# TensorE projects before it forms the output product in the attention steps, and GpSimd splits the weights

## The reference

```python
q = (x @ wq).reshape(B, T, H, Dh)
c_kv = x @ w_down
kv_up = (c_kv @ w_up).reshape(B, T, H, 2 * Dh)
k, v = (kv_up[..., :Dh], kv_up[..., Dh:])
q = _apply_rope(q, 0)
k = _apply_rope(k, 0)
scores = jnp.einsum('bqhd,bkhd->bhqk', q, k) * scale
scores = jnp.where(causal[None, None, :, :], scores, -jnp.inf)
attn = jax.nn.softmax(scores, axis=-1)
out = jnp.einsum('bhqk,bkhd->bqhd', attn, v).reshape(B, T, H * Dh)
return out @ wo
```

## Time and profile before

| | us |
|---|---|
| median of 3 runs (1430.68 to 1434.95) | 1431.06 |
| the profiled execution | 1435.23 |
| its span | 1433.2 |
| TensorE busy in the span | 1360.4 (95%) |
| VectorE busy | 1006.6 (70%) |
| ScalarE busy | 606.8 (42%) |
| GpSimd busy | 564.9 (39%) |

### The profile page before, as it was taken

How to read it: one execution, slowest core, us unless ns; L and a number is a source line. 1 busy time by engine, 2 the same in 40 slices (tenths; PEclk the granted TensorE clock), 3 DMA queues, 4 the chain that set the end, 5 groups by cost and what they waited for, 6 DMA issues and landing times.

```text
span 1433.2 us, 24788 instructions
## 1 busy us (share of the span) xinstructions
PE 1360.4 (95%) x8292; PEld 1114.6 (78%) x8292; DVE 1006.6 (70%) x2533; ACT 606.8 (42%) x1490; POOL 564.9 (39%) x488
## 2 busy tenths in 40 slices
PE   8998999999999999889999999999999999997995
PEld 7777787888888878668877788788788888874664
DVE  5797989898989898865564567566557657886225
ACT  4554555555555555533333343343334333351232
POOL 3775555555555555200124123513513522304122
PEclk9999999999999999999999999999999999988998
DMA  6000000000000200120000010110020001677994
GB/s 187 1 12 1 12 0 11 0 11 0 11 0 11 65 0 1 20 68 1 0 2 0 31 51 9 36 54 9 16 73 7 8 16 41 169 261 242 288 267 133
DMA packets 67952, 76.16 MB, mean 53 GB/s; under 512 B 14189, under 2 KB 55173, under 8 KB 67877
## 3 DMA queue, kind: packets, MB, share of 16 engines
q1 hardware_dynamic: 56533, 58.36, 14.1%
q10 hardware_dynamic: 8560, 12.36, 2.9%
q0 software_dynamic: 2784, 4.46, 1.5%
HBM read 66.22 MB, written 8.95 MB: 52 GB/s over the span
## 4 chain that ended last, share of the span: by engine, by line
PE 39%; DVE 8%; POOL 3%; ACT 3%; issue 2%; DMA 1%; POOLq 0%; ACTq 0%; DVEq 0%
PE ps L1848 28%; PE ps L2215 2%; PE ps L2364 2%; PE ps L2442 1%; PE ps L2205 1%; PE ps L2128 1%; PE ps L2129 1%; PE ps L2133 1%; POOL wq L626 1%; POOL wo L626 1%; DVE hidT L1440 1%; POOL wo L621 0%; POOL wq L621 0%; POOL qk L694 0%; PE ps L2424 0%
## 5 line engine op out<-in xcount | busy, mean ns | idle before, releaser
L863 ACT ACTIVATE probs<-ps,nm 128x128 f32<-128x128 f32 (+3 forms) x256 | 135.3, 529 | 209.2 <-DVE nm L1269 209.2
L694 POOL TENSOR_TENSOR qk<-q,ksb 128x512 f32<-128x512 f32 x64 | 83.5, 1304 | 283.1 <-ACT q L977 210.9
L1994 PE MATMUL ps<-kT,qT 128*128 128x128 f32 (+3 forms) x512 | 160.5, 436 | 8.7 <-ACT probs L863 4.6
L1201 DVE TENSOR_TENSOR prod<-ps,rope_sb 128x1024 f32<-128x1024 f32 x128 | 155.2, 1215 | 7.5 <-PE ps L1848 7.5
L556 POOL TENSOR_TENSOR qT<-prod 64x512 f32<-64x512 f32 x64 | 81.9, 1280 | 144.4 <-DVE prod L1201 134.0
L1178 DVE TENSOR_TENSOR pT_low<-ps,pT 128x384 fp32r<-128x384 f32 (+2 forms) x256 | 104.6, 450 | 44.4 <-ACT pT L783 44.4
L1269 DVE CUSTOM_DVE_ANT_0 ps<-ps,causal 128x128 f32<-128x128 f32 (+3 forms) x256 | 122.5, 499 | 7.6 <-PE ps L1994 7.5
L556 POOL TENSOR_TENSOR kT<-prod 64x512 f32<-64x512 f32 x64 | 81.9, 1279 | 90.7 <-DVE prod L1201 79.4
L1333 DVE SCALAR_TENSOR_TENSOR acc<-ps,rinv,acc 128x256 f32<-128x256 f32 x256 | 105.9, 473 | 1.8 <-issue 1.4
L783 ACT ACTIVATE pT<-ps 128x384 fp32r<-128x384 f32 (+2 forms) x256 | 85.1, 415 | 51.8 <-PE ps L2031 51.4
L1848 PEld LDWEIGHTS ps<-kvo,qn 128*128 128x128 f32 x768 | 100.2, 191 | 8.3 <-DVE qn L1178 3.6
(11 more groups left out here) (298 smaller groups left out, 3066.0 us busy)
## 6 DMA issues: line engine op xcount, KB each, us to landing
eg<-in_L_ffn_w_gate_dram SPq DMA_DIRECT2D x16, 704.0 KB
eg<-in_L_ffn_w_up_dram SPq DMA_DIRECT2D x16, 704.0 KB
ed<-in_L_ffn_w_down_dram ACTq DMA_DIRECT2D x10, 640.0 KB
ksb<-ks_dram SPq DMA_DIRECT2D x16, 256.0 KB, 3.3
ed<-in_L_ffn_w_down_dram SPq DMA_DIRECT2D x6, 640.0 KB
rows_dram<-rows ACTq DMA_DIRECT2D x4, 640.0 KB, 8.1
acc<-in_L_attn_x_dram SPq DMA_DIRECT2D x4, 512.0 KB
wq_in<-in_L_attn_wq_dram SPq DMA_DIRECT2D x8, 256.0 KB, 2.9
```

The lines of the kernel that those rows point to most:

```text
L694: nc.gpsimd.tensor_tensor(qk[:], q3[:], ksb[b % 2][:], ALU.mult).then_inc(qk_ready, 1)
L863: nc.scalar.activation(probs[hh][:, off:off + (i + 1) * P], ps[:, BS + i % 2, 0:(i + 1) * P], ACT.Exp, bias=nm[:, hh, i:i + 1], scale=-1.0 ...
L1201: nc.vector.tensor_tensor(prod[parity][w][:], ps[:, BA:BA + 2, :], rope[:, w:w + 1, :].broadcast_to([P, 2, T]), ALU.mult).then_inc(product ...
L1994: pe.matmul(ps[:, bank, 0:(i + 1) * P], qT[:, hh, b, i * P:(i + 1) * P], kT[:, hh, b, 0:(i + 1) * P], start=True, stop=True).then_inc(scor ...
```

## The change

There are three parts. In the attention's steps, `project` moves in front of `project_out`. Work of splitting moves from ScalarE and VectorE to GpSimd: the rests of wq and wk in every pair but the last, and both halves of all FFN weights, which GpSimd does when its last rotation is done, with root(1) in their midst. The factor SCALE moves from wq to the maxima's pass, the wait for all of U_low in front of the loop becomes one for each pair, the statistics of the first sequence move from n = 2 and 3 to n = 4 and 5, and around the FFN some transposes and copies change places.

```diff
-        w0_pieces = [([h[:, k, w, :] for h in gu], gu_in[:, k, w, :]) for k in range(KD) for w in range(2)]
-        w0_pieces.insert(2, ([h[:] for h in la], la_in[:]))
+        w0_pieces = [([h[:, k, w, :] for h in gu], gu_in[:, k, w, :]) for w in (1, 0) for k in range(KD)]
+        w0_pieces.insert(1, ([h[:] for h in la], la_in[:]))
         w0_pieces.append(([h[:] for h in lb], lb_in[:]))
...
+            def weights_rest(o, whole, hi, turned, ready, count, signal):
+                pool.wait_ge(roped, 4 * turned)
+                pool.wait_ge(ready, count)
+                nc.gpsimd.tensor_tensor(o, whole, hi.bitcast(F32), ALU.subtract).then_inc(signal, 1)
+                pool.wait_ge(signal, count)
...
             def pair(g, first, last):
                 for n in range(STEPS - LOOK if last else STEPS):
                     b = (n + LOOK) // 2 % BATCH
-                    if last and n == 2:
-                        pool.wait_ge(roped, 4 * (g * STEPS + LOOK + n))
-                        root(1)
-                        pool.wait_ge(rstd_ready, 1)
+                    if n == 3 and not last:
+                        weights_rest(wq[1][:], wq_in[:], wq[0][:], g * STEPS + LOOK + n, wq_hi, g + 2, wq_lo)
+                    if n == 4 and not last:
+                        weights_rest(wk[1][:], wk_in[:], wk[0][:], g * STEPS + LOOK + n, wk_hi, g + 2, wk_lo)
...
             pool.wait_ge(roped, 4 * PROJECTIONS)
+            pool.wait_ge(gu_loaded, 32)
+            for m, (halves, whole) in enumerate(w0_pieces):
+                if m == 1:
+                    pool.wait_ge(la_loaded, 8 * 16)
+                if m == 3:
+                    root(1)
+                    pool.wait_ge(rstd_ready, 1)
+                if m == 5:
+                    pool.wait_ge(lb_loaded, 64)
+                one = ones[0:whole.shape[0], :]
+                if len(whole.shape) == 3:
+                    one = one.rearrange("p (a n) -> p a n", a=1)
+                nc.gpsimd.tensor_tensor(halves[0], whole, one.broadcast_to(list(whole.shape)), ALU.mult).then_inc(w0_hi, 1)
+                pool.wait_ge(w0_hi, w0_first + m + 1)
+                nc.gpsimd.tensor_tensor(halves[1], whole, halves[0].bitcast(F32), ALU.subtract).then_inc(w0_lo, 1)
+            pool.wait_ge(w0_lo, w0_first + 6)
             root(2)
             root(3)
...
-                nc.scalar.activation(wq[0][:], wq_in[:], ACT.Copy, scale=SCALE).then_inc(wq_hi, 1)
+                copy(wq[0][:], wq_in[:]).then_inc(wq_hi, 1)
...
                 act.wait_ge(ha_turned, b + 1)
                 copy(haT[:], ps[0:NL, 6, :]).then_inc(haT_ready, 1)
+                if not last:
+                    xa_halves(b + 1)
...
-                nc.vector.tensor_tensor_reduce(out=row, in0=row, in1=causal[:, T - (i + 1) * P:T], scale=-1.0, scalar=-MASKED,
+                nc.vector.tensor_tensor_reduce(out=row, in0=row, in1=causal[:, T - (i + 1) * P:T], scale=-SCALE, scalar=-MASKED,
...
-                if n == 3 and not last:
-                    split_wq(g + 1)
-                if n == 4 and not last:
-                    split_wk(g + 1)
                 if last:
-                    if n == 2:
+                    if n == 4:
...
                         dve.wait_ge(acc_added, 4 * s)
                         statistics(tiles(0), None)
-                    if n == 3:
+                    if n == 5:
                         dve.wait_ge(rstd_ready, 1)
...
-                    if n in w0_lo_at:
-                        for m in w0_lo_at[n]:
-                            halves, whole = w0_pieces[m]
-                            dve.wait_ge(w0_hi, w0_first + m + 1)
-                            rest(halves[1], whole, halves[0]).then_inc(w0_lo, 1)
...
+            dve.wait_ge(w0_lo, w0_first + 6)
             route0(0)
             take_weights()
             o_rest(STEPS * PAIRS - 1)
+            xa_rests(0)
             add(STEPS * PAIRS - 1, STEPS - 1)
-            xa_rests(0)
...
                 scores(2)
                 scores(3)
-                if first and n == 1:
-                    pe.wait_ge(ulo_ready, ulo_first + 1)
+                if n + LOOK < STEPS or not last_pair:
+                    project((n + LOOK) % 2, (n + LOOK) // 2 % BATCH, s + LOOK, g if n + LOOK < STEPS else g + 1)
+                if n == 1:
+                    pe.wait_ge(ulo_ready, ulo_first + g + 1)
                 if not (first and n == 0):
                     project_out(*before)
-                if n + LOOK < STEPS or not last_pair:
-                    project((n + LOOK) % 2, (n + LOOK) // 2 % BATCH, s + LOOK, g if n + LOOK < STEPS else g + 1)
...
             pair(0, True, False)
-            pe.wait_ge(ulo_ready, ulo_first + HEADS // 2)
...
+                if first:
+                    project_out(STEPS * PAIRS - 1, PAIRS - 1, STEPS - 1)
                 pe.wait_ge(xalo_ready, b * 2 + 2)
...
-                if not last_one:
-                    turn_xa(b + 1)
...
-                pe.wait_ge(ha_ready, b * TPB + TPB)
                 for i in range(TPB):
+                    if i == TPB - 1 and not last_one:
+                        turn_xa(b + 1, (0,))
+                    pe.wait_ge(ha_ready, b * TPB + i + 1)
                     last = pe.transpose(ps[0:NL, 6, i * P:(i + 1) * P], ha[:, i, :], ident[:])
                 last.then_inc(ha_turned, 1)
+                if not last_one:
+                    turn_xa(b + 1, (1,))
...
             base_products(0, 0, 1)
-            project_out(STEPS * PAIRS - 1, PAIRS - 1, STEPS - 1)
             base_products(0, 1, 1)
             turn_xa(0)
```

More of the change, by code:

```diff
@@ L360, in wait_gathered @@
                 engine.wait_ge(gathered[q], 16 * (GROUPS // 4))
-        w0_pieces = [([h[:, k, w, :] for h in gu], gu_in[:, k, w, :]) for k in range(KD) for w in range(2)]
-        w0_pieces.insert(2, ([h[:] for h in la], la_in[:]))
+        w0_pieces = [([h[:, k, w, :] for h in gu], gu_in[:, k, w, :]) for w in (1, 0) for k in range(KD)]
+        w0_pieces.insert(1, ([h[:] for h in la], la_in[:]))
         w0_pieces.append(([h[:] for h in lb], lb_in[:]))
-        w0_hi_at = {4: (0, 1), 5: (2, 3, 4), 6: (5,)}
-        w0_lo_at = {5: (0, 1), 6: (2,), 7: (3, 4, 5)}
         def x1_bank(b):
@@ L831, in _ @@
             u_high(0)
[L833 to L843, removed]
-                    halves, whole = w0_pieces[m]
-                    copy(halves[0], whole).then_inc(w0_hi, 1)
             def x1_halves(b):
@@ L894, in step @@
                     x1_halves(0)
-                if last and n in w0_hi_at:
-                    ffn_weights_halves(n)
             def pair(g, first, last):
@@ L909, in scores0 @@
                 if b == 0:
-                    act.wait_ge(w0_lo, w0_first + 6)
+                    act.wait_ge(w0_lo, w0_first + 3)
                 bank = logits_bank(b)
@@ L958, in ffn0 @@
                     scores0(b + 1)
-                    xa_halves(b + 1)
                 else:
@@ L1181, in split_wq @@
                 dve.wait_ge(wq_hi, g + 1)
-                nc.vector.scalar_tensor_tensor(out=wq[1][:], in0=wq_in[:], scalar=SCALE, in1=wq[0][:].bitcast(F32),
-                                               op0=ALU.mult, op1=ALU.subtract).then_inc(wq_lo, 1)
+                rest(wq[1][:], wq_in[:], wq[0][:]).then_inc(wq_lo, 1)
             def split_wk(g):
@@ L2055, in first_products, with turn_xa @@
                 last.then_inc(logits_ready, 1)
-            def turn_xa(b):
+            def turn_xa(b, which=(0, 1)):
                 pe.wait_ge(xa_ready, b * TPB + TPB)
                 pe.wait_ge(x1lo_ready, b * KD + KD)
-                for w in range(2):
+                for w in which:
                     for i in range(TPB):
@@ L2146, in ffn0 @@
                               skip_group_check=True).then_inc(ffn_ready, 1)
-            pe.wait_ge(w0_lo, w0_first + 3)
+            pe.wait_ge(w0_lo, w0_first + 2)
             first_products(0)
             pv_and(STEPS * PAIRS - 1, STEPS - 1)
-            pe.wait_ge(w0_lo, w0_first + 5)
+            pe.wait_ge(w0_lo, w0_first + 3)
             base_products(0, 0, 1)
-            project_out(STEPS * PAIRS - 1, PAIRS - 1, STEPS - 1)
             base_products(0, 1, 1)
```

## The result

| | kernel before | changed kernel |
|---|---|---|
| median, us | 1430.87 (1430.52 to 1434.95, 4 runs) | 1504.62 (1503.6 to 1506.92, 4 runs) |
| profiled execution, span, us | 1433.2 | 1502.8 |
| mean granted TensorE clock | 0.984 | 0.988 |

The ratio is 1.0511, 95% interval 1.0488 to 1.0533: slower by 73.8 us. Forecast were 1501.8 and a range of 1482 to 1516.

What follows compares the result with a forecast made beforehand. The prediction took the loop as bound by TensorE's own work, with VectorE nearly as full and exactly in time. Its terms summed to +70.7 us on the 1431.06 us median, giving 1501.8; own bounds 1488 to 1513, with rivals' edges 1482 to 1516.

Steps and rivals of the forecast that it cites:

- new order, 59 steps: Attention steps 1 to 59: projection in front of the output product costs 1.45 us each, +85.6 us (77 to 94).
- rests, U_low, statistics in the loop: Attention loop: wq/wk rests on GpSimd -4.8 us, U_low wait per pair -5.8, statistics out of step 58 -1.5.
- last pair to the FFN's first product: From R (576.47 us before) to the FFN's first product: R+41.4 instead of R+38.2, +3.2 us (-2 to +8).
- seam: First FFN product to first with xaT: 3.6 us idleness and 2.9 slow clock go, 1.0 comes; -5.5 (-3 to -6.5).
- order of ha, xa, haT: Four FFN blocks: haT some 0.4 us earlier, xaT's rests as much later; -0.5 us in all (+-1).
- The projection's place: Attention step, S its first scores: projection held until VectorE's second multiplication ends at S+5.44, loading at S+5.49 to S+5.57.
- The stall pulls the clock down: Rival, 4%: in the loop each step's gap lowers TensorE's clock, 1.4 us more each, 1585 us.
- Partial stall: Rival, 10%: stall only 0.9 to 1.2 us a step, pT found ready, transposes not waiting; 1469 to 1487 us.
- rotations end at about R+12.3, la lands at R+20.3, root(1) R+26.0: Last pair, from R (576.47 us before): GpSimd's rotations end, la's copy lands, GpSimd finishes root(1) after gu, la, gu.
- four x1 tiles, some 1.9 by the additions' 1.66: Last pair, VectorE behind root(1): x1 tiles 1.9 us, oT_low 0.7, so TensorE resumes at R+28.6.
- GpSimd's queue is later: Rival, 13%: last pair, stretched halves' passes or x1 awaiting the second gu move R+28.6 by 6 to 12; 1508 to 1514.
- 1 us of idleness stays: Seam to the FFN: TensorE waits for xa, the routing's result, with less work in front of it; 1 us.

Runs made afterwards that it cites:

- order_back: The changed kernel with only the order undone, the output product again in front of the projection: 1422.83 us, 0.9925 of the kernel before.
- o_rest_late: The changed kernel, order kept, with oT_low on VectorE behind both rotation multiplications instead of between them: 1441.73 us, 1.0061 of the kernel before.
- x1_alone: The changed kernel, but GpSimd waits with its next half until VectorE's four x1 tiles are done: 1499.84 us, 1.0464 of the kernel before.
- seam_alone: The kernel before with only the last output product moved behind the base products of the first FFN block: 0.9983 of the kernel before.
- back_root: The changed kernel with the output product again before the projection, and the last pair's root(1) before all six halves on GpSimd: 1410.14 us, 0.9843.

## Why the prediction was right

By its own terms, measured in the traces:

| term | predicted | measured |
|---|---|---|
| new order, 59 steps | +85.6 | +83.4 (T59, changed kernel against order_back) |
| rests, U_low, statistics in the loop | -12.1 | -10.9 (T59, order_back against before) |
| last pair to the FFN's first product | +3.2 | +7.3 |
| seam | -5.5 | -7.4 |
| order of ha, xa, haT | -0.5 | 0.0 |
| the layers behind | 0 | -2.7 |

*The projection's place* was right in mechanism and size: the held load at S+5.49 to S+5.57 came at S+5.45, oT_low and the second multiplication kept their times, and each step lost 1.39 with a second wait of 0.16, where 1.45 was taken. o_rest_late shows the cause by moving it. What made this foreseeable was one pair of rows: ready at S+5.61 for banks that were free at S+5.44. An engine that waits for nothing may only not wait because of what stands in front.

*"The stall pulls the clock down"* did not happen. The clock stayed at 1.00 around 59 gaps of about 1.04 us in 604 us. The Trainium skill, "TensorE: Matmul & The Clock Gate", section "A second HAM failure mode: psum-queue depth-cycling", tells of frequent short gaps between groups of matmuls and a clock that went up and down with them; gaps of this size and spacing did not do it here.

*"Partial stall"* did not happen either: in the held steps the additions are late, as the forecast said, and cost their 0.16.

*The last pair* is where the sum was off. Two steps of it: "rotations end at about R+12.3, la lands at R+20.3, root(1) R+26.0" held (R+12.2, R+20.2, R+25.8); "four x1 tiles, some 1.9 by the additions' 1.66" was mis-sized by 4.4 us. The additions take one input from PSUM, and GpSimd's passes don't touch them; the x1 tiles are of another kind, a tensor_scalar from SBUF to SBUF, so the row was no measure for them. x1_alone shows the cause. The rival *"GpSimd's queue is later"* had such a loss in this place (6 to 12), but by GpSimd being late; GpSimd was in time, and VectorE was held by it. TensorE resumed at R+32.8, and from there the FFN's first product came 12.7 later, as forecast (12.8).

*The seam* was mis-sized the other way: "1 us of idleness stays" was 0. Here the step left out that the halves were no longer in VectorE's queue in front of the route; seam_alone measures that wait at 2.91 when they are. The two errors, +4.1 and -1.9, are of opposite sign. The terms measured add to +69.7, the spans' difference but for rounding, against +70.7 in the forecast; the medians differ by 73.8, since the profiled execution of the kernel before lay above its median and that of the changed kernel didn't. So a part of the closeness is luck: five of the terms were off by 1.2 to 4.1 us, in both directions. And the forecast's own bounds (-8.6 and +8.4 for the loop, +-6 for the seams) add to 1487 to 1516, not to 1488 to 1513.

*Behind the seam* the forecast had -0.5 for the order of ha, xa and haT. From the first product with xaT to the last with haT it is 170.74 us before (634.65 to 805.39) and 170.71 after (706.99 to 877.70): nothing. The other 2.7 is not from the change: 2.2 of it lie in the router stage of the last layer, 22.43 us (1343.33 to 1365.76) against 24.58 (1271.07 to 1295.65) with the same instructions, at a mean granted clock of 0.93 where before it was 0.81. The stage's length does not follow the parts of the change: from the first transposes of `marked` to the same end it takes 35.95 us in the kernel before and 33.81 in the changed one, but 35.98 in order_back and 33.79 in back_root, which both have the old order in the attention. What decides when the clock comes back there stays open.

## What to carry to other kernels

Before moving a piece of work forward on the engine that sets the pace, look up when its banks or inputs are let go, and compare that with when the engine would now reach them: the piece in front may be free only because it lies over that wait, and the wait's end is another engine's instruction order, which may be the cheaper thing to change (here 63 of 82 us came back by moving one instruction of VectorE). Work given to an idle GpSimd is not free if VectorE has a tensor_scalar from SBUF to SBUF or a tensor_tensor of two SBUF tiles beside it; put such VectorE work where GpSimd rests. And a short piece that others wait for (the root of four columns) goes to the front of a queue of long ones: that was worth about 12 us, some 5 of them because the x1 tiles then fell into a rest of GpSimd's.

## What the hardware showed

VectorE's x1 tiles (tensor_scalar on SBUF, 128x256) took 1.38 us for four alone and 6.28 beside GpSimd's passes on SBUF. The first and the last of the four in the changed kernel:

```profile
674.82 1.52 DVE L1308 TENSOR_SCALAR acc<-acc,meanvar,rstd 128x256 f32<-128x256 f32 x1 [6.84 <-POOL rstd L562]
```

```profile
679.32 1.79 DVE L1308 TENSOR_SCALAR acc<-acc,meanvar,rstd 128x256 f32<-128x256 f32 x1
```

The first ends at 676.34, 0.14 behind the end of a GpSimd pass (674.87 + 1.33), the last at 681.11, 0.16 behind one (679.32 + 1.63). A tensor_tensor of 32 columns from two SBUF tiles took 1.94 us and ended 0.05 behind GpSimd's pass; alone it takes 0.19. GpSimd's own passes did not stretch in these cases: over 688 columns 1.33 to 1.38 and 1.63 to 1.67 us.

VectorE's instructions with one input in PSUM were not held. The additions to acc are the best case: 244 of the 256 lie beside a pass of GpSimd by more than 0.12 us, and all 256 take between 0.471 and 0.484 us. The rotation's multiplications lie beside one only now and then, because the rotation waits for them; where one does (406.20, beside GpSimd's rest of wq at 405.66) it takes 1.22, as in the earlier trace rows. Nor was every instruction on SBUF alone held. The statistics of the same acc tiles ran beside a pass over gu, the two together in 0.74 us, while the tensor_scalar of four columns behind them took 0.28 in place of 0.17 and ended 0.03 behind that pass:

```profile
661.10 0.74 DVE L1260 BATCH_NORM_STATS2 stat<-acc 128x6 f32<-128x256 f32 x2
662.29 0.28 DVE L1265 TENSOR_SCALAR vareps<-meanvar 128x4 f32<-128x4 f32 x1
```

```profile
661.21 1.33 POOL L625 TENSOR_TENSOR gu<-gu_in,ones 128x688 fp32r<-128x688 f32 x1
```

And it goes the other way too. In the second layer VectorE's tensor_tensor of two SBUF tiles began 0.26 us ahead of a pass of GpSimd, kept its 1.22 us, and the pass took 2.11 where the 64 of its line have a mean of 1.30:

```profile
932.05 1.22 DVE L1414 TENSOR_TENSOR acc<-acc,bo_sb 128x1024 f32<-128x1024 f32 x1
```

```profile
932.31 2.11 POOL L714 TENSOR_TENSOR qk<-q,ksb 128x512 f32<-128x512 f32 x1 [4.43 <-ACT q L982]
```

By this, the two engines don't share the way to SBUF in slices; one waits until the other's instruction ends. The Trainium skill, "SBUF — State Buffer", section "Who interferes with whom", says so: the pair of ports that VectorE shares with GpSimd is locked for a whole instruction, for VectorE instructions in a mode that uses both ports or with two SBUF inputs, and not for one with at most one SBUF input outside those modes. The trace agrees with it for the tensor_tensor (1.94 against 0.19), the additions (unchanged) and the statistics (unchanged). For the tensor_scalar it agrees in the holding (6.28 against 1.38); that the tiles ran in a mode with both ports no row names. There is a sign of it: behind the end of GpSimd's pass an x1 tile of 256 columns needed 0.14 to 0.16 us, about 0.6 ns a column, and a held tensor_tensor of 512 columns (qs, 1050.60 to 1053.41, beside a pass that ended at 1052.85) needed 0.56, about 1.1 ns a column.
